# A centered product in three passes of split operands, placed two column blocks later in the down product

## What is computed

```
q, k1, k2, v1, v2 = x + x @ W.T + b          (five times, split into heads)
S1 = k1^T v1 / n;  S2 = k2^T v2 / n;  S12 = S1 * S2
out = q@S1 * mean(v2) * g1 + sum(S12) * g2 + q@S2 * mean(v1) * g3 + q@S12 * g4
out = layernorm(out) * ln_g + ln_b;  out = out @ Wo.T + bo
x1 = layernorm(x + out)
```

```
h = relu(x1 @ w1[0] + b1[0]);  y2 = x1 + h @ w2[0] + b2[0]
result = layernorm(x1 + layernorm(y2) * gamma + beta)
```

## Time and profile before

| | us |
|---|---|
| median of 3 runs | 204.87 |
| lowest, highest | 204.83, 205.17 |
| the profiled execution | 204.72 |
| its span in the profile | 203.0 |
| share of TensorE busy, of VectorE | 94%, 78% |
| share of ScalarE, of GpSimd | 64%, 70% |

### The profile page before, as it was taken

One profiled execution on the slowest core, in us unless ns is written; L12 is line 12 of the kernel. 1 busy time (PEld: TensorE's weight loads), 2 busy tenths in 40 slices (PEclk: granted clock), 3 DMA queues, 4 the chain that ended last, 5 costly groups with the idle time before them and its releaser, 6 DMA issues.

```text
span 203.0 us, 4316 instructions
## 1 busy us (share of the span) xinstructions
PE 191.2 (94%) x1381; PEld 174.8 (86%) x1381; DVE 157.6 (78%) x471; ACT 129.2 (64%) x386; POOL 141.2 (70%) x190
## 2 busy tenths in 40 slices
PE   6899999999999999999999999999999999999920
PEld 6788997989898999999997989898989899987820
DVE  0186745987869887898879896989698969897683
ACT  0342538372859665975758675967597759786852
POOL 8526662676489838986599759985998598877350
PEclk9999999999999999999999999999999999999985
DMA  5999501200001000101001300100010101011012
GB/s 151 238 243 288 143 0 27 58 0 5 0 0 55 37 15 5 53 0 52 3 16 51 117 2 0 53 28 28 0 55 2 52 3 52 2 52 40 15 53 103
DMA packets 12624, 10.64 MB, mean 52 GB/s; under 512 B 713, under 2 KB 10458, under 8 KB 12602
## 3 DMA queue, kind: packets, MB, share of 16 engines
q1 hardware_dynamic: 11944, 9.32, 15.2%
q0 software_dynamic: 352, 0.92, 2.5%
q10 hardware_dynamic: 306, 0.13, 0.2%
HBM read 6.17 MB, written 4.20 MB: 51 GB/s over the span
## 4 chain that ended last, share of the span: by engine, by line
PE 85%; DVE 6%; issue 3%; ACT 2%; POOL 2%; DVEq 0%; POOLq 0%; ACTq 0%
PE up_ps L1024 26%; PE down_ps L1024 25%; PE z_ps L1024 14%; PE prep_ps L1024 12%; PE turn_ps L1177 4%; PE turn_ps L1148 3%; DVE st L793 1%; DVE down_ps L844 1%; POOL y2g L548 1%; POOL y L552 1%; DVE z_ps L904 1%; ACT res L667 1%; DVE y2n L800 1%; DVE res L1001 0%; DVE y L986 0%
## 5 line engine op out<-in xcount | busy, mean ns | idle before, releaser
L1024 PE MATMUL down_ps<-w_sb,hT 128*128 128x128 f32 x480 | 58.9, 276 | 0.1
L1024 PEld LDWEIGHTS down_ps<-w_sb,hT 128*128 128x128 f32 x480 | 56.4, 192 | 0.7 <-ACT hT L685 0.3
L685 ACT ACTIVATE hT<-up_ps,cols 128x512 f32<-128x512 f32 x64 | 42.2, 682 | 5.2 <-PE up_ps L1024 5.0
L667 ACT ACTIVATE res<-y,nb,rstd 128x128 f32<-128x128 f32 x60 | 24.8, 483 | 6.6 <-POOL nb L516 5.9
L574 POOL TENSOR_TENSOR x1b<-x,b_rows 128x512 f32<-128x512 f32 x16 | 20.5, 1284 | 10.6 <-DVE x L800 10.6
L1024 PE MATMUL up_ps<-x1T_hi,w_hi 128*128 128x512 f32 x64 | 26.1, 408 | 0.0
L1024 PE MATMUL up_ps<-x1T_lo,w_hi 128*128 128x512 f32 x64 | 25.4, 398 | 0.0
L1024 PE MATMUL up_ps<-x1T_hi,w_lo 128*128 128x512 f32 x64 | 25.3, 395 | 0.0
L548 POOL TENSOR_TENSOR y2g<-y2n,gamma_rows 128x512 f32<-128x512 f32 x15 | 19.2, 1281 | 4.9 <-DVE y2n L800 4.9
L800 DVE TENSOR_SCALAR x<-z_ps,st,rstd 128x128 f32<-128x128 f32 x64 | 21.9, 405 | 0.1
L634 ACT ACTIVATE z_sq<-z_ps 128x128 f32<-128x128 f32 x64 | 16.8, 270 | 7.6 <-PE z_ps L1024 7.6
(11 more groups left out here) (170 smaller groups left out, 418.3 us busy)
## 6 DMA issues: line engine op xcount, KB each, us to landing
X<-in_L_attn_x SPq DMA_DIRECT2D x8, 512.0 KB, 8.7
out<-res SPq DMA_DIRECT2D x15, 256.0 KB, 2.0
V_all<-V_dram SPq DMA_DIRECT2D x6, 128.0 KB, 3.1
w_sb<-in_L_ffn_w POOLq DMA_DIRECT2D x2, 256.0 KB, 8.4
out<-res SPq DMA_DIRECT2D x2, 128.0 KB, 2.2
w_raw<-in_L_attn_Wv ACTq DMA_DIRECT2D x2, 64.0 KB, 2.7
w_raw<-in_L_attn_Wk SPq DMA_DIRECT2D x2, 64.0 KB, 3.9
w_raw<-in_L_attn_Wo POOLq DMA_DIRECT2D x1, 64.0 KB, 3.0
```

The lines of the kernel that those rows point to most:

```text
L667: last = act.activation(res[buf][:, t, :], y3[buf][:, t, :], ACT.Identity, scale=rstd4[:, t:t + 1], bias=nb4[:, t:t + 1])
L685: act.activation(hT[:, k, :], up_ps[k % len(up_ps)][:, :], ACT.Relu, bias=cols[:, 5 + k:6 + k]).then_inc(relu_out, 1)
L1024: return pe.matmul(o, lhsT, rhs, start=start, stop=stop)
```

## The change

Four tiles are added: `PT_hi` and `PT_lo`, the two parts of `PT`, and `both_hi` and `both_lo`, the two parts of `center`. GpSimd splits `center` once, at step 0. For b >= 2 ScalarE writes `PT_hi` in place of `PT_sb`, and VectorE writes `PT_lo` in the middle of the four instructions that normalize x1. `centered(b)` for b >= 2 waits for `PT_lo` and is made of six float32r matmuls of 128x256 in place of two float32 ones. It stands ahead of tile t = 3, not in the middle of tile t = 2. Batches 0 and 1 are made as before.

```diff
+            def split_both():
+
+                pool.wait_ge(zw_ready, 1)
+                pool.tensor_copy(both_hi[:, :, :], center[:, :, :]).then_inc(both_split, 1)
+                pool.wait_ge(both_split, 1)
+                pool.tensor_tensor(both_lo[:, :, :], center[:, :, :], both_hi[:, :, :].bitcast(f32), ALU.subtract).then_inc(both_split, 1)
+
...
                 if st.n == 0:
                     split_A()
+                    split_both()
...
-                act.activation(PT_sb[:, :], prep_ps[:, 0:XW], ACT.Copy).then_inc(PT_out, 1)
+                act.activation(PT_sb[:, :] if b < 2 else PT_hi[:, :], prep_ps[:, 0:XW], ACT.Copy).then_inc(PT_out, 1)
...
+            def PT_rest(b):
+
+                wait(dve, PT_out, b + 1)
+                dve.tensor_tensor(PT_lo[:, :], prep_ps[:, 0:XW], PT_hi[:, :].bitcast(f32), ALU.subtract).then_inc(PTlo_out, 1)
+
...
-                    normalize(x1, y1_tile, st2, rstd2, x1_out)
+                    normalize(x1, y1_tile, st2, rstd2, x1_out, (lambda: PT_rest(st.prepared())) if st.prep and n >= 0 else None)
...
+                if b >= 2:
+
+                    wait(pe, PTlo_out, b - 1)
+                    pe.wait_ge(both_split, 2)
+                    hi, lo = (t[:, :, :].rearrange("p j c -> p (j c)") for t in (both_hi, both_lo))
+                    for part, pt in ((slice(0, 256), lambda t: t[:, 0:C]),
+                                     (slice(256, 512), lambda t: t[:, C:C + 1].to_broadcast([128, 128]))):
+                        mm(prep_ps[:, part], pt(PT_hi), hi, start=True, stop=False)
+                        mm(prep_ps[:, part], pt(PT_hi), lo, start=False, stop=False)
+                        last = mm(prep_ps[:, part], pt(PT_lo), hi, start=False, stop=True)
+                    last.then_inc(p_done, 1)
+                    return
...
-                            if t == 2 and k == 2 and st.prep:
+                            if t == 3 and k == 0 and st.prep:
                                 centered(st.prepared())
```

More of the change, by code:

```diff
@@ L123, in build @@
         PT_sb = sb("PT_sb", [128, XW])
+        PT_hi = sb("PT_hi", [128, XW], f32r)
+        PT_lo = sb("PT_lo", [128, XW], f32r)
+        both_hi = sb("both_hi", [128, 2, 128], f32r)
+        both_lo = sb("both_lo", [128, 2, 128], f32r)
         PQ_hi = sb("PQ_hi", [128, 512], f32r)
@@ L231, in build @@
         rows_done = sem("rows_done")
+        both_split = sem("both_split")
+        PTlo_out = sem("PTlo_out")
         A_split = sem("A_split")
```

## The result

The changed kernel takes 205.74 us, the median of 7 runs (205.22 to 206.23), where the kernel before took 204.87 us in the same series (7 runs, 204.69 to 205.28). The ratio is 1.0035 with a 95% interval of 1.002 to 1.0051, so it is slower by about 0.72 us; the two medians lie 0.87 us apart (1.0042), which the interval holds too. The forecast was 205.84 us, a ratio of 1.0047. The profiled execution of the changed kernel took 206.14 us, with a span of 204.4 us, and the mean granted clock of TensorE is the same (0.986 of full speed, 0.984 before).

A forecast was written before the change was run, and what follows sets the result against it. TensorE, busy 94%, was taken to bound the kernel, with two points hanging on the chain behind the centered product. 5 x 0.18 + 0.07 = 0.97 us more turned 204.87 into 205.84 us; range 205.0 to 206.5.

The forecast's parts named there:

- The work on TensorE: Centered product in six even steps: six matmuls take 0.71 us instead of 0.95, gaining 0.24 a step, 1.42 us in all.
- the prediction's other working: Centered product priced from float32's four passes: three passes cost 0.32 us, ending 0.06 us earlier, forecast's sum about 0.35 smaller.
- The broadcast operand: Rival at the centered product: new matmuls need more than one pass, 2.6 us a step, over 214 us; chance 0.01.
- The end of the product: Centered product, step 2: ends at 59.02, 0.21 us later than 58.81, shifting VectorE's and ScalarE's chains by as much.
- rows 4 and 7: Profile rows for the up product's fourth part and its load waiting for the ReLU; spare time before was 0.03 us only.
- PT_lo: VectorE's subtraction amid x1's normalizations: takes 0.29 us, ends at 57.94; the product may start at 58.10, due 58.15.
- the larger loss: Rival: PT_lo takes 0.42 us or starts late, the product starts 0.08 us later; 206.3 us, chance 0.12.
- The three holes: TensorE waits before product's fourth matmul (0.20 us given back), x1T_lo (0.07 late) and the up product's fourth part (0.18).
- The sum of the steps: Six changed places: 5 x 0.18 + 0.07 = 0.97 us more, the 0.07 in step 7.
- What is free: GpSimd's one split of center, at most 1.5 us, hides before a 5.63 us idle; PT_hi costs what PT_sb did.
- The faster case: Rival: the chain does not set TensorE's points, so the whole lighter product comes through; 203.45 us, chance 0.08.
- The smaller loss: Rival: the ReLU's wait is not tight, only x1T_lo counts, 6 x 0.07 = 0.42; 205.29 us, chance 0.14.

The follow-up runs named there:

- one pass: The changed kernel with only the first of the three passes in the centered product, the two correcting passes left out; 202.91 us, ratio 0.9897 to the kernel before.
- late copy: The kernel before with a one-column ScalarE activation ahead of the copy PQ_hi, nothing changed on TensorE; 205.36 us, ratio 1.0013.
- the move alone: The kernel before with its float32 centered product put ahead of tile 3 of the down product; 207.34 us, ratio 1.0112.
- the two halves: The changed kernel with the product's second half written to another PSUM bank and PQ_hi copied in two halves; 203.63 us, ratio 0.9926 to the kernel before.
- the old place: The changed kernel with its three-pass centered product back in the middle of tile 2; 205.71 us, ratio 1.0036 to the kernel before.
- the kernel with the moved root: The changed kernel with ScalarE's root put behind two of the four squares in odd steps from 3; 204.84 us, ratio 0.9994 to the kernel before.

## Why the prediction was right, point by point

**The work on TensorE**: six matmuls 0.118 us apart, 0.71 us in all, as foretold. The row of `product` was the right price: 0.35 us for three passes, not the 0.32 us of the prediction's other working. The broadcast operand costs nothing extra.

**The end of the product**: 0.204 us later than before after the mark, where 0.21 was foretold. The experiments put this term to the proof. These four kernels leave the chain behind the product as it is and move its end by different amounts ("a step" is the mean of the five distances):

| kernel | end of the product, us | a step, us |
|---|---|---|
| one pass | -0.26 | -0.29 |
| late copy (PQ_hi's chain) | +0.06 | +0.035 |
| the change | +0.204 | +0.176 |
| the move alone | +0.37 | +0.314 |

The step follows the end of the product, less 0.03 to 0.05 us, though TensorE's work per step is 0.71 us less in the first and unchanged in the second. The 0.03 us is the spare time that the forecast read between rows 4 and 7. The rule ends where TensorE's own work or wait is the later one, as in the two halves and at the old place.

**PT_lo**: it lasts 0.293 us (0.29 foretold) in all six places, as the tile's own view in the changed kernel has it (ns min/median/max):

```profile
L832 DVE TENSOR_TENSOR PT_lo<-prep_ps,PT_hi x6: 293/294/294, 58.4 to 167.3; 128x130 fp32r<-128x130 f32 x6
```

The product starts when it was due. So the larger loss (0.42 us) does not occur. At the old place the 0.16 us from the producer's end to the matmul can be checked: PT_lo ends 1.26 us after the mark, and the first matmul runs at 1.41.

**The three holes**: in `product` 0.19 us (0.20 foretold), at x1T_lo 0.065 us late (0.07), at the fourth part of the up product 0.176 us late (0.18). The weight loads of the changed kernel, which answer to the earlier trace rows:

```profile
63.44 0.19 PEld L1043 LDWEIGHTS up_ps<-x1T_lo,w_hi 128*128 128x128 f32 x1 [0.27 <-DVE x1T_lo L961]
...
65.18 0.19 PEld L1043 LDWEIGHTS up_ps<-x1T_hi,w_hi 128*128 128x128 f32 x1 [0.29 <-issue]
```

The first ReLU ends at 65.07, the load is 0.11 us behind it, and the matmul 0.11 behind that.

**The sum of the steps**: 0.97 us was foretold and 1.06 measured (0.88 + 0.18). The five distances from mark to mark grow by 0.16, 0.19, 0.18, 0.17 and 0.18 us. The third holds steps 7 and 8. In step 7 only the 0.07 us of x1T_lo is seen, as foretold. Most of the rest is in step 8, at a place that the forecast had left out. VectorE's timeline there, before and then after:

```profile
116.55 0.17 DVE L869 RECIPROCAL rstd<-std 128x4 f32<-128x4 f32 x1
116.75 0.73 DVE L800 TENSOR_SCALAR y2n<-down_ps,st,rstd 128x128 f32<-128x128 f32 x2
```

```profile
117.68 0.17 DVE L888 RECIPROCAL rstd<-std 128x4 f32<-128x4 f32 x1
117.97 0.73 DVE L814 TENSOR_SCALAR y2n<-down_ps,st,rstd 128x128 f32<-128x128 f32 x2
```

The second instruction starts 0.04 us behind the first one's end before, and 0.13 us after, and `E_sb`, for which TensorE waits, stands behind it. This happens once, in step 8, in each of the six kernels with split operands, the two of halves too, and in none of the five float32 ones. What it is likely to be stands in the last section.

**The tail**: here the sum was off. From the last matmul to the end it takes 0.34 us less, which no step of the forecast had. Without it the time would be 1.06 us up, a ratio of 1.0052, just outside the measured interval. So the nearness of 205.84 to 205.74 is partly luck: the steps lost 0.09 us more than the sum said, the tail gave 0.34 back, and the median of 205.74 lies some 0.15 us above what the ratio gives. VectorE's and GpSimd's timelines in the tail, before:

```profile
193.91 0.17 DVE L1007 SCALAR_TENSOR_TENSOR rstd<-st,rstd 128x2 f32<-128x2 f32 x1
194.35 0.76 DVE L793 BATCH_NORM_STATS2 st<-y 128x6 f32<-128x256 f32 x2 [0.27 <-POOL y L552]
```

```profile
192.80 1.27 POOL L552 TENSOR_TENSOR y<-y2g,x1beta 128x512 f32<-128x512 f32 x1
```

and after:

```profile
195.67 0.18 DVE L1026 SCALAR_TENSOR_TENSOR rstd<-st,rstd 128x2 f32<-128x2 f32 x1
195.87 0.76 DVE L807 BATCH_NORM_STATS2 st<-y 128x6 f32<-128x256 f32 x2
```

```profile
194.57 1.26 POOL L566 TENSOR_TENSOR y<-y2g,x1beta 128x512 f32<-128x512 f32 x1
```

In both, GpSimd's y ends 0.02 us ahead of the moment at which VectorE is free (194.07 and 194.08; 195.83 and 195.85). Before, the statistics start 0.29 us after y's end, after, 0.03 us: this is a wait of 0.26 us that has gone. The other 0.09 us lies behind VectorE's last instruction, where the last stores are; its cause is open. For the first see the last section.

**What is free**: GpSimd's split takes 0.40 + 0.73 us in a stretch in which it idles 4.45 us afterwards (5.63 before), so it costs nothing, as foretold.

**The rivals.** The faster case asked that VectorE's sum wait for the down product and not for PQ_hi's second half. That is not so in the changed kernel, where the sum at 61.30 has no idle time. The kernel of two halves has the slack that this rival asked for (its sum comes 0.57 us earlier after the mark, 3.33 in place of 3.90), and gives what the rival would: TensorE's gain. The smaller loss (only x1T_lo counts) is what the kernel with the moved root shows, and the changed kernel is not that. The matmuls do run in one pass for the broadcast operand.

## What to carry to other kernels

Before a product is made lighter or moved, write down when its last matmul ends, follow the chain behind it to the next point at which the matrix engine needs it, and take the spare time at that point from the trace: here it was 0.03 us, and an engine without a visible hole lost nearly all that the chain was late. When a lighter product brings nothing, let the copy of its result start on the first half: here each of the two alone gave nothing, and both gave 0.7%. Where a root that waits stands ahead of work that does not wait, let that work go first if its own end is waited for; where nothing waited for it, the same edit brought nothing.

## What the runs showed of the hardware that was not expected

An activation of 128x1 lasts 0.17 us in the trace and delays the one behind it by only 0.07 us.

The same program takes up to 0.7 us more or less until its first loads have landed: the mark in step 2 stands at 56.70 us before, at 57.38 and 57.34 in two kernels that are the same up to there. Two profiled executions of kernels this close must be compared from a mark behind the start.

At two places VectorE starts late in some kernels and not in others, always alike within a kind. In the tail the statistics start 0.27 to 0.29 us behind y's end in all five kernels with the float32 product and 0.03 us behind it in all six with split operands, though VectorE's instruction before them ends 0.02 us behind y in both kinds. And in step 8 y2n starts 0.04 us behind the reciprocal in the first five and 0.13 us in the other six. The two together were worth 0.26 - 0.09 = 0.17 us here, a quarter of the net change of 0.7 us.

The traces hold a likely cause. The late instruction is the 576th entry of VectorE's list in the five kernels and the 320th in the six (semaphore entries of the trace counted), 256 entries apart. The list is three entries longer in the six by step 8 and six entries longer by the tail, one `PT_lo` for each even step, so another instruction falls on that place. And the queue that the page calls "q14 instruction" starts a transfer of 8192 bytes shortly behind each late start: 0.65 to 0.93 us behind the statistics in the five kernels, 0.66 to 1.00 us behind y2n in the six. Where the same instruction is in time it is not so: in the tail of the six the last such transfer starts 3.05 to 3.08 us ahead of the statistics, and in step 8 of the five one starts 1.12 to 1.42 us behind y2n. So it looks as if VectorE loses up to 0.26 us where its list goes over into a new block of instructions just behind a short one, and a change that adds a few instructions to the list moves that place. No run adds instructions alone, so this is not shown; a kernel before with six idle entries more in VectorE's list would test it.
